# Keys and queries of batches 2 to 7 as three fp32r products of rounded parts and remainders

## The reference, cut to what matters

```python
x = L0_attn_x                                   # (8, 512, 128) float32
x = x + attention(layernorm(x), W_qkv, b_qkv, W_out, b_out)
x = x + moe(layernorm(x), w_router, w_up, w_gate, w_down, ws_up, ws_gate, ws_down)

# attention: 16 heads of 8, causal, a window of 32 keys
qkv = x @ W_qkv + b_qkv
scores = einsum('bnid,bnjd->bnij', q, k) / sqrt(8)
scores = where((i - j < 0) | (i - j >= 32), -inf, scores)
out = einsum('bnij,bnjd->bnid', softmax(scores), v)
...
return out @ W_out + b_out

# moe: 8 choices, the best one of them counts (7 experts, the eighth is empty), hidden 512
exp_out = (x @ w_up * silu(x @ w_gate)) @ w_down
...
shared = x @ ws_up * silu(x @ ws_gate) @ ws_down
```

## Time and profile before

| | us |
|---|---|
| median of 3 runs | 351.09 (350.62 to 353.26) |
| the profiled execution | 354.27 |
| its span | 352.5 |
| PE busy / DVE / ACT / POOL | 319.2 / 219.6 / 148.9 / 186.9 |
| mean granted clock of TensorE | 0.971 of full speed |

### The profile page before, as it was taken

The page is one execution under the profiler, slowest core; times in us unless marked ns, Lnnn a source line. Parts: engine busy times, 40 slices in busy tenths (PEclk is TensorE's granted clock), DMA queues, the critical chain, the costliest instruction groups (busy, mean ns, idle before and its releaser), DMA issues. The chain is left out here.

```text
span 352.5 us, 12260 instructions
## 1 busy us (share of the span) xinstructions
PE 319.2 (91%) x4914; PEld 251.7 (71%) x4914; DVE 219.6 (62%) x456; ACT 148.9 (42%) x267; POOL 186.9 (53%) x280
## 2 busy tenths in 40 slices
PE   8889969998998989996899999995999999999970
PEld 8646545665665665894778888784888888888860
DVE  6798767887987888689473333452455555555520
ACT  3345424543443664662142222331545455555520
POOL 7898654444579626596477744341333334333430
PEclk9999998999999999999699999998999999999996
DMA  7943231324133231598012211223434333333200
GB/s 199 353 102 76 69 81 52 71 69 105 41 107 70 63 69 33 206 378 213 25 61 106 103 61 62 61 57 55 74 68 86 69 65 69 78 75 74 63 16 0
DMA packets 53529, 32.49 MB, mean 92 GB/s; under 512 B 26448, under 2 KB 47700, under 8 KB 53474
## 3 DMA queue, kind: packets, MB, share of 16 engines
q1 hardware_dynamic: 48992, 23.18, 27.0%
q0 software_dynamic: 2880, 6.43, 5.3%
q10 hardware_dynamic: 1602, 2.10, 1.9%
HBM read 13.72 MB, written 11.95 MB: 73 GB/s over the span
## 5 line engine op out<-in xcount | busy, mean ns | idle before, releaser
L654 POOL DMA_INDIRECT out<-y,xn_base x38 | 37.4, 983 | 72.1 <-DVE y L1244 72.1
L1592 PE MATMUL psB<-down_sb,Pr 128*128 x304 | 41.3, 280 | 5.3 <-DVE y L1244 4.6
L1233 DVE TENSOR_TENSOR Pr<-psS,PT 128x512 f32<-128x512 f32 x38 | 26.3, 693 | 30.7 <-PE psS L1578 29.5
L950 DVE STREAM_TRANSPOSE PT<-Pr 128x1024 f32<-128x1024 f32 x32 | 39.4, 1240 | 8.6 <-ACT Pr L738 8.3
L738 ACT ACTIVATE Pr<-psS 128x1024 f32<-128x1024 f32 x32 | 32.7, 1028 | 28.5 <-PE psS L1330 28.5
L1049 DVE TENSOR_TENSOR hT<-psS,PT 128x512 f32<-128x512 f32 x32 | 22.1, 690 | 33.6 <-PE psO L1483 26.2
L1592 PEld LDWEIGHTS psB<-down_sb,Pr 128*128 128x128 f32 x304 | 37.7, 195 | 5.9 <-issue 5.9
L816 ACT ACTIVATE PT<-psS 128x512 f32<-128x512 f32 x32 | 19.1, 598 | 51.2 <-PE psS L1471 40.8
L895 DVE TENSOR_REDUCE row_max<-psS 128x16 fp32r<-128x1024 f32 x32 | 37.3, 1208 | 0.0
L858 ACT ACTIVATE PT<-psS 128x512 f32<-128x512 f32 x38 | 22.7, 598 | 28.0 <-PE psS L1572 27.2
L1318 PE MATMUL psS<-Kx,Qx 32*32 32x256 f32 x1024 | 34.1, 377 | 0.0
(11 more groups left out here) (206 smaller groups left out, 693.5 us busy)
## 6 DMA issues: line engine op xcount, KB each, us to landing
sorted_rows<-pad_rows SPq DMA_DIRECT2D x9, 528.0 KB, 5.7
xn_base<-sorted_rows SPq DMA_DIRECT2D x38, 66.0 KB, 1.9
xs<-sorted_rows SPq DMA_DIRECT2D x152, 16.0 KB
rows<-in_L_attn_x SPq DMA_DIRECT2D x8, 256.0 KB, 6.2
VD_even<-V SPq DMA_DIRECT2D x28, 72.0 KB
VD_odd<-V SPq DMA_DIRECT2D x28, 72.0 KB
gate_sb<-in_L_ffn_w_gate ACTq DMA_DIRECT2D x1, 1792.0 KB, 12.0
Kx<-K SPq DMA_DIRECT2D x28, 64.0 KB, 2.3
```

The costliest lines, as they stand in the source:

```text
L654: pool.indirect_dma_start(out=out_list, out_offset=bass.IndirectOffsetOnAxis(tok_u[:, r, :], 0), in_=y[:, r, :], in_offset=None, bounds_ch ...
L950: nc.vector.transpose(PT[:, half, :], Pr[:, half, :]).then_inc(pt_done, 1)
L1233: nc.vector.tensor_tensor(hs[:, r % 2, :], psS[:, r % 2, 0:512], sg[:, r % 2, :], ALU.mult).then_inc(eh_done, 1)
L1592: last = mm(psB[:, 0:D], hsT[:, r % 2, c * P : (c + 1) * P], down_flat[:, bass.ds(start + c * D, D)], start=(c == 0), stop=(c == NC - 1),)
```

## The change

The weights `wqk_sb` are split once, on GpSimd, into `wqk_hi` (rounded to fp32r) and `wqk_lo` (the remainder), before its loop over pairs. From batch 2 on, ScalarE reads `psA` a second time and writes the rounded part `xnT_hi`; GpSimd subtracts it from `xnT` into `xnT_lo`. Each of keys and queries becomes three products accumulated in one bank: `wqk_lo` with `xnT_hi`, `wqk_hi` with `xnT_hi`, `wqk_hi` with `xnT_lo`. The third waits for the subtraction. Batches 0 and 1 and all values stay in fp32.

```diff
+    SPLIT_FROM = 2
...
+        wqk_hi = sb("wqk_hi", [P, 2, D], f32r)
+        wqk_lo = sb("wqk_lo", [P, 2, D], f32r)
...
+        xnT_hi = nc.alloc_sbuf_tensor_at("xnT_hi", [P, T], f32r, offset=place["hT"] + 4 * 2 * T)
+        xnT_lo = nc.alloc_sbuf_tensor_at("xnT_lo", [P, T], f32r, offset=place["hT"] + 4 * 3 * T)
...
+            def low_part(n):
+                pool.wait_ge(xnT_ready, n + 1)
+                pool.wait_ge(xnT_hi_ready, n - SPLIT_FROM + 1)
+                pool.tensor_tensor(xnT_lo[:, :], xnT[:, :], xnT_hi[:, :].bitcast(f32), ALU.subtract).then_inc(
+                    xnT_lo_ready, 1
+                )
+
+            def split_projection():
+                pool.wait_ge(wqk_ready, 2)
+                pool.tensor_copy(wqk_hi[:, :, :], wqk_sb[:, :, :]).then_inc(wqk_hi_ready, 1)
+                pool.wait_ge(wqk_hi_ready, 1)
+                pool.tensor_tensor(wqk_lo[:, :, :], wqk_sb[:, :, :], wqk_hi[:, :, :].bitcast(f32), ALU.subtract).then_inc(
+                    wqk_lo_ready, 1
+                )
+
+            split_projection()
             G1, G2 = 5 * TPB, (B - 1) * TPB
             EARLY, SPLITS = 5 * PPB, PPB
             for p in range(EARLY):
                 b, h = divmod(p, PPB)
+                if h == 1 and SPLIT_FROM <= b + 2 < B:
+                    low_part(b + 2)
                 residual(p)
                 if h == 0 and b + 3 < B:
                     normalise(b + 3)
...
             add_bias(B - 1)
             normalise_rows(0, 1)
+            low_part(B - 1)
             residual(EARLY + 1)
...
                 nc.scalar.copy(xnT[:, :], psA[:, :]).then_inc(xnT_ready, 1)
+                if n >= SPLIT_FROM:
+                    act.wait_ge(q_done, n)
+                    nc.scalar.copy(xnT_hi[:, :], psA[:, :]).then_inc(xnT_hi_ready, 1)
...
+            def rounded_products(bank, which, n, done):
+
+                pe.wait_ge(wqk_lo_ready, 1)
+                pe.wait_ge(xnT_hi_ready, n - SPLIT_FROM + 1)
+                mm(bank[:, :], wqk_lo[:, which, :], xnT_hi[:, :], start=True, stop=False)
+                mm(bank[:, :], wqk_hi[:, which, :], xnT_hi[:, :], start=False, stop=False)
+                pe.wait_ge(xnT_lo_ready, n - SPLIT_FROM + 1)
+                mm(bank[:, :], wqk_hi[:, which, :], xnT_lo[:, :], start=False, stop=True).then_inc(done, 1)
+
             def queries(n):
                 pe.wait_ge(xnT_ready, n + 1)
-                mm(psA[:, :], wqk_sb[:, 0, :], xnT[:, :], start=True, stop=True).then_inc(q_done, 1)
+                if n < SPLIT_FROM:
+                    mm(psA[:, :], wqk_sb[:, 0, :], xnT[:, :], start=True, stop=True).then_inc(q_done, 1)
+                else:
+                    rounded_products(psA, 0, n, q_done)
...
                 if n >= 2:
                     pe.wait_ge(v_ready, n - 1)
-                mm(psB[:, :], wqk_sb[:, 1, :], xnT[:, :], start=True, stop=True).then_inc(k_done, 1)
+                if n < SPLIT_FROM:
+                    mm(psB[:, :], wqk_sb[:, 1, :], xnT[:, :], start=True, stop=True).then_inc(k_done, 1)
+                else:
+                    rounded_products(psB, 1, n, k_done)
```

More of the change, by code:

```diff
@@ L220, in windowed_attention_top1_moe_kernel @@
         norm_done, xt_done, xnT_ready = sem("norm_done"), sem("xt_done"), sem("xnT_ready")
+        wqk_hi_ready, wqk_lo_ready = sem("wqk_hi_ready"), sem("wqk_lo_ready")
+        xnT_hi_ready, xnT_lo_ready = sem("xnT_hi_ready"), sem("xnT_lo_ready")
         q_done, k_done, v_done = sem("q_done"), sem("k_done"), sem("v_done")
```

## The result

The changed kernel takes 382.21 us in the median of 4 runs (379.19 to 387.71), against 352.17 us for the kernel before; the ratio is 1.084, with an interval of 1.073 to 1.095. I had forecast 365.2 us. The direction was right; the size was not, and the time lies above my range.

What follows compares the result with a forecast made beforehand. TensorE, busy for 91%, was taken as the bound, with queries on the path and keys almost hidden. Delays +12.1, queries -1.2 and clock +3.2 gave +14.1 us on the profiled execution, or 365.2 us from the median; range 360.0 to 371.5.

Steps and rivals of the forecast that it cites:

- The products: Attention stage on PE: three fp32r products save 0.2 us per query, -1.2 us over six; keys, hidden behind the exponential, 0.
- ScalarE's copy at no cost: ScalarE's second read of psA takes about 0.6 us and ends a microsecond before the exponential, so it costs nothing.
- The delays by batch: Third keys product waits for GpSimd's remainder, delaying batches 2 to 7; the delays add up to 12.1 us.
- TensorE's clock: Attention stage: two of four new idle times bring half clock, 1.6 us lost each, +3.2 us; bounds 0 and 6.5.
- (b): Waits come in full: batch 3 waits too (+2.7 us) and the clock falls each time (+6.5); 371.2 us; chance 0.2.
- (a): The waits at the keys come but the clock holds; 362.0 us; chance 0.2.
- (c): Remainder is there before PE's third keys product, so nothing waits; 347.9 us, or 349.9 if only queries save; chance 0.03.
- (d): ScalarE's rounded copy also pushes the exponentials, up to +3.5 us; 368.7 us; chance 0.07.

Runs made afterwards that it cites:

- e1: Changed kernel, but GpSimd subtracts before normalising the batch after next and splitting gate weights (batch 7: right after the second rstd); 350.96 us, ratio 1.002.
- e7: Changed kernel, but keys stay one fp32 product in all batches and only queries are three rounded products; subtraction still late; 351.93 us, ratio 1.000.
- e2: Changed kernel without GpSimd's subtraction of the activations; the third product reads the rounded part again, without a wait; 352.04 us, ratio 1.003.
- e6: Changed kernel, but the wait stands before all three products and PE then repeats the first keys product 12 times; 391.58 us.
- e3: Changed kernel with copy, subtraction and wait kept, but behind the wait keys and queries are one fp32 product each; 388.03 us, ratio 1.092.
- e4: Changed kernel, but PE repeats the first keys product 2 to 11 times per batch while GpSimd works its queue off; 368.37 us, ratio 1.044.
- e8: As e1, but batch 7's subtraction stands ahead of the residual and the second rstd; 349.13 us, ratio 0.993.
- e9: e8's GpSimd order, copies, subtractions and waits, but keys and queries are one fp32 product each behind the wait; 362.19 us, ratio 1.005.
- e5: Changed kernel, but GpSimd subtracts between the normalisation and the weight splits (batch 7 as in e1); 351.20 us, ratio 0.998.

## Why the prediction was wrong, point by point

*The products.* Right in size at the full clock: I took 0.2 us per query, e1 shows 0.16 at all six. In the changed kernel's profile the queries all lay in half-clock stretches and took 0.53 us more than before instead. That the keys bring nothing, as I said, no run tests by itself.

*ScalarE's copy at no cost.* Right: 0.59 us each, and e7 isn't slower.

*The delays by batch.* The place and the queue were right, and the total was, partly by luck. Forecast 2.5, 0, 2.8, 1.2, 2.9 and 2.7 us for batches 2 to 7; the idle times are 1.94, 0.58, 2.69, 0.58, 2.46 and 3.36, together 11.6 against 12.1. Only one of the four long ones lies in the 2.5 to 2.9 us that I named. Three shorter ones are made up for by batch 7's. There GpSimd itself stood idle for 1.92 us before the residual at 138.46, just behind ScalarE's eviction of the projection; it had no such wait in the kernel before. That the low clock had put the projection off is likely, not shown.

*TensorE's clock, the term of the sum that was mis-sized.* I put it at +3.2 us, with bounds of 0 and 6.5: two of four waits followed by a stretch like that of the earlier trace rows, 1.6 us lost in 3.4. The loss per microsecond was about right; both the count and the length were wrong. From the first keys product of batch 2 to the last projection the changed kernel takes 174.24 - 34.26 = 140.0 us, and e1, which differs by the order on GpSimd alone, 136.58 - 33.75 = 102.8. Of these 37.2 us, 11.6 - 1.4 = 10.2 are longer waits; I put the other 27 down to the 68 us at half clock, 0.40 us in each, where the earlier trace rows gave 1.6 in 3.5. There were six stretches, and each lasted 6.8 to 13.7 us. These are two profiles. The medians are only 382.2 - 351.0 = 31.2 us apart, so there the clock's part is some 21 us (an estimate, with the waits as in the profiles), still three times my bound. And the two stretches that began before their wait, at batches 3 and 5, are 27 of the 68 us, or 11 of the 27 us lost at 0.40 each, an estimate again. e2 had stretches of 3.4 and 10.2 us at these batches with no wait at all, so what part of them is the late subtraction's stays open.

My upper bound of 6.5 us took the stretch of the earlier trace rows for the longest there can be. The trace of the kernel before already had a longer one, 6.8 us in the shared stage behind a wait of 2.57 us, and in its second half PE is busy for all of the time:

```profile
168.23:171.64 3.41, 1.95 (x8) 1.20 (x7) 2.90 (x8) 1.11 (x2) 0.64 (x1) 0.52 0.00 0
171.64:175.05 3.41, 3.41 (x18) 3.41 (x18) 0.00 (x0) 0.00 (x0) 2.70 (x3) 0.50 0.15 44
```

Four stretches of that length would have given an upper bound twice mine, still too low. What did have that the others hadn't? PE was doing a keys matmul at that moment, dense work, and e6 shows that this matters; behind the new wait only one dense product and the two of the shift are left before the small matmuls begin. In e3 the fp32 keys, too, were mostly not enough, so one cannot count on them either.

*The rivals.* (b), full waits and a fall of the clock at each of the four long ones, was the nearest and still 11 us short, by the same bound. (a), the clock holds, is what e4 nearly made true by other means. (c), nothing waits, was wrong for this order; e1 and e8 are what it would have been, 349 to 351 us beside my 347.9 to 349.9. (d) didn't happen.

## What to carry to other kernels

When an in-order engine is given one more operation that a critical engine waits for, where it stands in that engine's queue decides, not how long it takes: 1.27 us of subtraction cost 8% behind three other operations and nothing measurable ahead of them. An idle time of TensorE has to be priced with what follows it: with twelve dense repeats behind it a fall of the clock lasted 3.4 us here, ahead of scores and projection mostly 6.8 to 13.7 us. A single stretch in a trace is no upper bound for this; look through the other stages for longer ones.

## What the runs showed of the hardware that I had not expected

- Of two kernels in which the same product waits for the same late subtraction, the one whose TensorE repeats a matmul in the meantime and throws the result away is 14 us faster in the median (368.4 against 382.2, in two sessions; the ratios are 1.044 and 1.084).
- The clock stayed at half for 10.2 us while PE's records show it busy for all of the 10.2 us (batch 4 above, and e2). Busy time in the page doesn't tell whether the clock will rise.
- Issue stalls of PE are followed by low stretches as waits for data are, but their length doesn't decide it. Those of 1.73 and 2.00 us in the changed kernel, 1.78 and 2.20 in e2, 1.85 in e4, 1.89 in e9 and 2.68 in the kernel before were followed by one within 1.5 us; those of 1.96 in e1, 2.01 in e7, 2.04 in e5, 2.05 in e8 and 2.32 in e9 were not.
- Of the waits for the remainder without such a stall just ahead, those of 1.40 us (e1) and 1.42 us (e4) left the clock up and that of 1.74 us (e4) didn't. What decides stays open.
